# A two-layer graph network with routed experts: routed rows moved into the next layer's staging memory, a fourth load buffer, and turned queries and keys worked out among the values

## The reference, cut to what matters

```python
x = x + gnn0(layernorm(x), src, dst)        # 80000 edges, 4 heads, leaky relu, softmax per target, relu
x = x + moe(layernorm(x))                   # 8 experts, each node goes to its top 2
x = x + gnn1(layernorm(x), src, dst)        # 80000 edges + own loops, 8 heads of 32, then a dense block
x = x + last_layer(layernorm(x))            # routed by the mean, gelu

def moe(tokens):
    rw, re = top_k(softmax(tokens @ router_w.T), 2)
    rw = rw / rw.sum(-1)
    for e in range(8):
        y = gelu(tokens @ w1[e] + b1[e]) @ w2[e] + b2[e]
        out = out + combine[:, e:e + 1] * y      # combine is zero but for the two chosen experts
    return out                                    # starts as tokens

# head of gnn1
Qh = (x @ Wq + bq).reshape(N, 8, 32);  Kh = (x @ Wk + bk).reshape(N, 8, 32)
Vh = (x @ Wv + bv).reshape(N, 8, 32)
s = einsum('nhc,nhc->nh', Qh, Kh) / sqrt(32)      # one score per node and head
```

## Time and profile before

| | |
|---|---|
| Three runs | 2370.11, 2376.10, 2381.61 us (median 2376.10) |
| The profiled execution | 2364.94 us, span 2363.2 us, mean granted TensorE clock 0.844 |
| PE, PEld busy | 1577.8 us (67%), 1284.0 us (54%) |
| DVE busy | 1667.0 us (71%) |
| ACT busy | 826.1 us (35%) |
| POOL busy | 1464.3 us (62%) |
| Four fills of `answered` (page, part 6) | 5632.0 KB each, 45.2 us from issue to landing |
| 27 loads of `sent`, 27 stores of `answered` | 256.0 KB each, 2.7 and 2.0 us |

### The profile page before, as it was taken

How to read it: one execution, slowest core, us unless ns; L and a number is a source line. 1 busy time by engine, 2 the same in 40 slices (tenths; PEclk the granted TensorE clock), 3 DMA queues, 4 the chain that set the end, 5 groups by cost and what they waited for, 6 DMA issues and landing times. The chain is left out here.

```text
span 2363.2 us, 38672 instructions
## 1 busy us (share of the span) xinstructions
PE 1577.8 (67%) x9941; PEld 1284.0 (54%) x10019; DVE 1667.0 (71%) x2748; ACT 826.1 (35%) x2126; POOL 1464.3 (62%) x1570
## 2 busy tenths in 40 slices
PE   4597015788766665377564999404688898758498
PEld 4476014566544444376563777403566666547387
DVE  6688714899755557665563888997578888686676
ACT  4365100000000002455301334106467777525464
POOL 4777747777777773616554777777777777700060
PEclk9799557999887787599786999856899999879799
DMA  5646696666433435333342666764566666430101
GB/s 159 213 139 228 211 404 189 215 208 199 142 106 106 106 106 161 136 121 114 101 130 103 195 213 191 244 194 140 163 217 212 202 217 213 108 100 1 45 10 35
DMA packets 145357, 372.17 MB, mean 157 GB/s; under 512 B 39577, under 2 KB 66473, under 8 KB 131715
## 3 DMA queue, kind: packets, MB, share of 16 engines
q0 software_dynamic: 66144, 180.94, 26.9%
q1 hardware_dynamic: 64447, 161.13, 19.4%
q10 hardware_dynamic: 14692, 29.23, 3.4%
HBM read 262.50 MB, written 108.70 MB: 157 GB/s over the span
## 5 line engine op out<-in xcount | busy, mean ns | idle before, releaser
L1349 DVE TENSOR_TENSOR ms_msg<-e_ring,ms_ps_w 128x1040 f32<-128x1040 f32 (+1 forms) x352 | 437.7, 1244 | 334.7 <-SPq L1267 280.3
L1368 PE MATMUL ms_ps_m<-ms_msg,ms_pick 128*128 128x260 f32 x1408 | 400.2, 441 | 230.6 <-DVE ms_msg L1349 147.3
L893 POOL DMA_INDIRECT e_ring<-table,e_index x465 | 440.2, 947 | 163.0 <-issue 137.1
L1368 PEld LDWEIGHTS ms_ps_m<-ms_msg,ms_pick 128*128 128x128 f32 x1408 | 298.4, 220 | 332.3 <-issue 280.7
L1368 PE MATMUL ms_ps_m<-ms_msg,all_xn 128*128 128x272 f32 x1408 | 364.3, 420 | 89.4 <-issue 71.1
L893 POOL DMA_INDIRECT e_ring<-table,l_index x369 | 353.1, 957 | 114.4 <-issue 111.2
L1368 PEld LDWEIGHTS ms_ps_m<-ms_msg,all_xn 128*128 128x128 f32 x1408 | 273.2, 201 | 180.3 <-issue 126.4
L935 POOL DMA_INDIRECT w_staged<-table,l_stage_index x256 | 267.3, 1044 | 104.6 <-issue 59.2
L768 PE MATMUL sc_ps_e<-sc_keys,sc_hot 125*128 125x100 bf16 (+1 forms) x3840 | 292.0, 230 | 21.3 <-DVE all_xn L713 17.7
L768 PEld LDWEIGHTS sc_ps_e<-sc_keys,sc_hot 125*128 125x128 bf16 x3840 | 256.4, 98 | 68.6 <-DVE all_xn L713 24.9
L671 ACT ACTIVATE sc_rows<-sc_ps_b 125x512 bf16<-125x512 f32 x320 | 173.2, 595 | 294.6 <-remote 171.3
(11 more groups left out here) (497 smaller groups left out, 2793.3 us busy)
## 6 DMA issues: line engine op xcount, KB each, us to landing
...
answered<-l_low_fill ACTq DMA_DIRECT2D x4, 5632.0 KB, 45.2
...
all_acc<-sent SPq DMA_DIRECT2D x27, 256.0 KB, 2.7
answered<-all_acc SPq DMA_DIRECT2D x27, 256.0 KB, 2.0
```

The lines of the kernel that those rows point to most:

```text
L893: pool.indirect_dma_start(out=g.ring[:, slot * QUAD + i // GT, i % GT, :], out_offset=None, in_=s.table[:, :], in_offset=bass.IndirectOffs ...
L1349: dve.tensor_tensor(msg[:, b, :, 0:R].rearrange("p t (h o) -> p t h o", h=H), ring[:, bass.ds(slot, 1), :, :].rearrange("p a t (h o) -> p ...
L1368: mm = pe.matmul(ps_m[b][:, 0:W], pick[:, b, t, :], msg[:, b, t, :], start=t == 0, stop=t == GT - 1)
```

## The change

Four things are changed together.

- `sent` and `answered` are gone. One memory, `s.routed`, takes both, and it is the front part of `s.ahead`, the staging memory. An answer overwrites the rows it was computed from, so the memory needs no zeros: the four fills on ACT and the nine on SP are removed, the wait for the latter too. Regions are `NP` rows apart, and a third row of the table tells where a tile's answer goes.
- There are 4 load buffers instead of 3, and 2 answer buffers instead of 3. The additions of the blocks' own rows (`own_added`) stand ahead of the loop; in the loop only statistics and variance of block 0 remain, and ACT's part of its normalization stands behind the loop. Block 4's return gathers have a buffer and a semaphore of their own.
- Queries and keys are computed turned: the weights' 128 columns are the stationary operand and 512 nodes the moving one, 24 matmuls for a block. ACT adds the query's bias, DVE adds the key's bias and multiplies by the query (2 instructions for a block), and PE sums per head by 8 matmuls with a mask (`of_head`).
- This work is placed block by block among the values, on PE, ACT and DVE. There are three banks for turned rows and two for values in place of four and four. POOL's own code behind the return gathers is unchanged.

```diff
+def staged_rows(s, width):
+
+    quad = P * QUAD * GT * width
+    return s.ahead[0:s.ahead.shape[0] // quad * quad].rearrange("(a p f) -> a p f", p=P, f=QUAD * GT * width)
...
-            if most is None:
-                rows = 8 * SENT_ROWS // ANSWER_FILLS
-                for i in range(ANSWER_FILLS):
-                    into = s.answered[i * rows:(i + 1) * rows, :].rearrange("(p r t) d -> p r (t d)", p=P, t=2)
-                    act.dma_start(into, s.low_fill[:, 0:2 * D].unsqueeze(1).broadcast_to([P, into.shape[1], 2 * D])).then_inc(s.answers_filled, 16)
...
+    DUMMY = X * NP
+    GOT = 4
...
+        got = spare[:, 1024:1024 + GOT * 2 * D].rearrange("p (a t d) -> p a t d", a=GOT, t=2)
+        answer = spare[:, 3072:3072 + 2 * 2 * D].rearrange("p (a t d) -> p a t d", a=2, t=2)
...
+        second_back = [late_back[:, :, :] if b == NB - 1 else back for b in range(NB)]
...
-        turn_banks = [banks[0:2], banks[2:4]]
-        v_banks, qk_banks = banks[4:8], [banks[4], banks[5], banks[6], banks[7]]
...
                     pool.wait_ge(answered, tiles_needed)
-                    if b > BY_POOL:
-                        pool.wait_ge(combined, SUB * b)
+                    back, landed = second_back[b], s.last_returned if b == NB - 1 else returned
...
+                def load(q):
+
+                    row = table_value(ENG.SP, 0, q, DUMMY)
+                    if q >= GOT:
+                        sp.wait_ge(tile_turned, q - GOT + 1)
+                    sp.dma_start(got[:, q % GOT, :, :].rearrange("p t d -> p (t d)"), tile_rows(s.routed, row)).then_inc(got_in[q % GOT], 16)
+
+                def passed(q):
+
+                    sp.wait_ge(stored[q % 2], 16 * (q // 2 + 1))
+                    sp.sem_inc(answered, 1)
+
...
-                sp.dma_start(s.sent[DUMMY:DUMMY + TT, :].rearrange("(p t) d -> p (t d)", t=2), zeros).then_inc(fills_in, 16)
-                sp.wait_ge(held_kept, 1)
...
-                    sp.dma_start(tile_rows(s.sent, count + e * SENT_ROWS), zeros).then_inc(fills_in, 16)
...
-                sp.wait_ge(fills_in, 16 * (X + 1))
                 sp.wait_ge(sent, 16 * 2 * NT)
...
+                for q in range(GOT):
...
-                    if q + 3 < TILES:
-                        load(q + 3)
+                    if q + GOT < TILES:
+                        load(q + GOT)
                     sp.wait_ge(y_kept, q + 1)
                     if q >= 1:
                         passed(q - 1)
-                    sp.dma_start(tile_rows(s.answered, table_value(ENG.SP, 0, q, DUMMY)),
-                                 answer[:, q % 3, :, :].rearrange("p t d -> p (t d)")).then_inc(stored[q % 3], 16)
+                    sp.dma_start(tile_rows(s.routed, table_value(ENG.SP, 2, q, DUMMY + TT)),
+                                 answer[:, q % 2, :, :].rearrange("p t d -> p (t d)")).then_inc(stored[q % 2], 16)
                 passed(TILES - 1)
...
+                        if a >= 2:
+                            pe.wait_ge(v_ready, a - 1)
+                        product(w_v, a, v_banks[a % 2][:, 0:D]).then_inc(v_sum, 1)
+
+                def queries_and_keys(b):
+                    cols = slice(b * TB, (b + 1) * TB)
+                    for f in range(KB):
+                        part = slice(f * P, (f + 1) * P)
+                        for weights, bank, summed, freed in ((w_q, q_bank, q_sum, q_ready), (w_k, k_bank, k_sum, product_ready)):
+                            if b * KB + f >= 1:
+                                pe.wait_ge(freed, b * KB + f)
+                            split_products(pe, bank[:, :], [((weights[0][:, kb, part], weights[1][:, kb, part]), (w.xt[0][:, kb, cols], w.xt[1][:, kb, cols]))
+                                                            for kb in range(KB)]).then_inc(summed, 1)
+
+                def node_scores(b):
+                    pe.wait_ge(product_ready, (b + 1) * KB)
+                    if b >= 1:
+                        pe.wait_ge(score_ready, b)
+                    for q in range(SUB):
+                        for f in range(KB):
+                            first = q * H + f * (H // KB)
+                            dot = pe.matmul(dot_bank[:, first:first + H // KB], qk[:, b % 2, f, q * P:(q + 1) * P], w.of_head[:, :], start=True, stop=True)
+                    dot.then_inc(dot_ready, 1)
...
                 pe.wait_ge(y_kept, TILES)
                 pe.wait_ge(qkv_lows, 3)
                 turn_rows(0)
-                for b in range(NB):
-                    if b + 1 < NB:
-                        turn_rows(b + 1)
-                    values(b)
-                for a in range(NT):
-                    scores(a)
+                turn_rows(1)
+                values(0)
+                queries_and_keys(0)
+                values(1)
+                node_scores(0)
+                turn_rows(2)
+                queries_and_keys(1)
+                values(2)
+                node_scores(1)
+                queries_and_keys(2)
+                turn_rows(3)
+                values(3)
+                node_scores(2)
+                turn_rows(4)
+                queries_and_keys(3)
+                values(4)
+                node_scores(3)
+                queries_and_keys(4)
+                node_scores(4)
 
             @block.scalar
...
                         tile_high_part(q + 2)
                     if q + 1 < TILES:
                         activated(q + 1, expert_of[q + 1])
-                    if q == EARLY_TILE:
-                        deviation2(0)
-                        normalized2(0)
-                deviation2(1)
-                normalized2(1)
-                act.wait_ge(y_kept, TILES)
-                for b in range(NB):
-                    highs(b)
-                    if b + 2 < NB:
-                        deviation2(b + 2)
-                        normalized2(b + 2)
+
+                def queries(b):
+                    for f in range(KB):
+                        act.wait_ge(q_sum, b * KB + f + 1)
+                        if b >= 2:
+                            act.wait_ge(product_ready, (b - 2) * KB + f + 1)
+                        act.activation(query[:, b % 2, f, :], q_bank[:, :], ACT.Identity, bias=w.bias_cols[:, 0, f:f + 1]).then_inc(q_ready, 1)
+
+                def second_norm(b):
+                    deviation2(b)
+                    normalized2(b)
+
+                second_norm(0)
+                second_norm(1)
+                highs(0)
+                highs(1)
+                queries(0)
+                second_norm(2)
+                highs(2)
+                queries(1)
+                queries(2)
+                second_norm(3)
+                highs(3)
+                second_norm(4)
+                queries(3)
+                highs(4)
+                queries(4)
 
             @block.vector
...
+                def add_own(first, end):
+                    for b in range(first, end):
+                        dve.tensor_tensor(s.x[:, blocks[b], :], s.x[:, blocks[b], :], s.xn[:, blocks[b], :], ALU.add).then_inc(own_added, 1)
+
                 expert_of = [w1_low_part(0), w1_low_part(1)]
+                add_own(0, 3)
                 tile_low_part(0)
                 tile_low_part(1)
+                add_own(3, NB)
                 hidden_low_part(0)
...
-                    if q < NB:
-                        dve.tensor_tensor(s.x[:, blocks[q], :], s.x[:, blocks[q], :], s.xn[:, blocks[q], :], ALU.add).then_inc(own_added, 1)
-                    elif q < NB + 3:
-                        qkv_low(q - NB)
+                    if 4 <= q < 7:
+                        qkv_low(q - 4)
                     elif q == EARLY_TILE:
                         dve.wait_ge(combined, SUB)
                         statistics(0, stats2_ready)
                         variance(0, stats2_ready, second_gap)
-                        offsets(0, std2_ready, shift2_ready)
...
+                def products(b):
+                    for f in range(KB):
+                        dve.wait_ge(k_sum, b * KB + f + 1)
+                        dve.wait_ge(q_ready, b * KB + f + 1)
+                        if b >= 2:
+                            dve.wait_ge(dot_ready, b - 1)
+                        dve.scalar_tensor_tensor(out=qk[:, b % 2, f, :], in0=k_bank[:, :], scalar=w.bias_cols[:, 1, f:f + 1], in1=query[:, b % 2, f, :],
+                                                 op0=ALU.add, op1=ALU.mult).then_inc(product_ready, 1)
+
+                def keep_scores(b):
+                    dve.wait_ge(dot_ready, b + 1)
+                    dve.tensor_scalar(score[:, blocks[b], :].rearrange("p a h -> p (a h)"), dot_bank[:, 0:SUB * H], float(O) ** -0.5, None,
+                                      ALU.mult).then_inc(score_ready, 1)
...
+                offsets(0, std2_ready, shift2_ready)
+                for i in range(2):
+                    dve.wait_ge(stored[i], 16 * len(range(i, TILES, 2)))
...
+                norm(1)
+                lows(0)
```

(23 more changed lines are left out.)

172 lines of the change are left out of this document (66 added, 106 removed).

## The result

| | before | changed |
|---|---|---|
| Median | 2381.61 us (11 runs, 2367.91 to 2388.31) | 2359.44 us (11 runs, 2345.37 to 2362.99) |
| Ratio changed / before | | 0.9908, 95% interval 0.9885 to 0.9930 |
| Profiled execution | 2364.94 us, span 2363.2, clock 0.844 | 2352.64 us, span 2350.7, clock 0.839 |
| Last gather of layer 0's message passing | 908.29 | 886.75 |
| First turning of a tile (S) | 1002.21 | 977.84 |

The change made the kernel 22 us faster in the medians (2381.61 - 2359.44; by the interval of the ratio 17 to 27), near the -24 that was forecast; the forecast time was 2352 us, from a median before of 2376.1. The profile shows 26.3 us gained up to the barrier and 12.5 at the end.

What follows compares the result with a forecast made beforehand. POOL's stall of 21.75 us, then its own issues, were taken to bound layer 0's message passing, and a chain the stretch behind the experts' loop; -21.4 - 2 - about 0.5 = -24 gave 2352 us from 2376.1, range 2328 to 2368.

Steps and rivals of the forecast that it cites:

- The fills: Layer 0's message passing: without the four fills on ACT, POOL's stall goes; -21.4 us, bounds -57 and -10.
- The rule on issue times: Skill's rule that initiating a DMA is usually small; by it removing ACT's fills gives nothing, sum -2 instead of -24.
- Start of the loop: Ahead of the experts' tile loop: SP's fill wait goes, first turn at 1001; -1.2 us, between 0 and -2.6.
- The loop: Experts' tile loop: a fourth load buffer issues loads one iteration earlier; iterations 3.45 us, last answer at 1103, bounds 1098 and 1114.
- The way back: POOL's return gathers and combination behind the experts: 27.7 us per block, block 0 from 1039, block 2 through at T + 19.
- T: End of the last answer in the experts' tile loop; 1144.1 before, forecast 1103, 41 us earlier.
- The tail: Behind the loop: interleaved queries and keys lengthen PE's path; rows land at T + 92, 1195 instead of 1196.75, bounds +72 and +104.
- Sum: Whole kernel: -21.4 - 2 - about 0.5 = -24 us, 2341 profiled, 2352 against the median 2376.1.
- Behind the rows: POOL's 24 gathers and 20 scatters after the table's rows land: unchanged at 56.7 us; earlier scores give nothing.
- B: Rival: short tail, PE at full clock, normalizations done beside it; rows at T + 72 to T + 80, 2336 us; chance 0.24.
- C: Rival: small gain, T at 1114, tail at its upper bound or layer 0 giving half; -5 to -13, 2367 us; chance 0.17.
- D: Rival: loop gains nothing because SP's one queue holds loads behind stores; T near 1143, +17, 2393 us; chance 0.05.

Runs made afterwards that it cites:

- scores last: Changed kernel with the turned queries and keys of all blocks behind the last values on PE, ACT and DVE; ratio to before 0.9805.
- normalizations first: Changed kernel, DVE combining and normalizing blocks 3 and 4 once landed, values 3 and 4 ahead of later queries and keys; 2315.71 us, ratio to before 0.9777.
- block 2 on DVE: As the kernel with normalizations first, with block 2 combined by DVE instead of POOL; ratio to before 0.9786.

## Why the prediction was right, point by point

- **The fills.** Forecast -21.4, measured -21.5 at the last gather of the stage. PE's first sums run from 314.71 to 321.2 (forecast: near 323), ahead of POOL's issue at 331.79, so nothing waits. Shown by the stall that comes and goes with the fills (21.75, none, 21.47). The pass ends near 896, as said. The price was read from POOL's wait and not from DVE's 49.5 or ACT's 56.4, and that reading decides the forecast.
- **The rule on issue times.** The prediction set the row against the Trainium skill (DMA: Bandwidth & Descriptors, section Issuing engines are not separate DMA queues). Both hold: a first fill is issued in 0.61 us, "small relative to the DMA itself", which lands after 25.1; of four in a row the later ones took 12.8 to 26.6. The sum by that rule is -2.5 with the prediction's own terms, not the -2 that it gives.
- **Start of the loop.** Forecast -1.2, measured -2.8 (24.37 less 21.54): 1.6 ahead of the last scatter (995.12 to 971.95), 1.2 behind it. Nothing told the parts of the first apart.
- **The loop.** Forecast 102 us, measured 98.6, at the lower bound: 10.8 + 26 x 3.37 is 98.4, and the 97 that the prediction has is its slip. Iterations took 3.29 us instead of 3.37, and the mean clock was 0.96 where the prediction went on from 0.88. Of the 43.3 us gained the fourth load buffer carries 31.2 (129.8 without it) and the moved normalization 2.9; the other 9 were not taken apart.
- **The way back.** Forecast block 0 at S + 38 and block 2 through at T + 19, measured S + 38.2 and T + 24.2 (1100.66): T was 3.4 earlier than forecast, and the first block took 30.9 us instead of 27.7, its first gather at 1.00 and one at 1.39 us, and its eight additions 7.6 us (5.6 in block 2).
- **The tail.** Forecast T + 92, measured T + 94.2. The steps fell as walked: block 1 turned at +8.4 (+9), block 2 at +29.4 (+30), combination 3 at +48.2 (+50.2, from 58.6 less 8.45), block 3 turned at +56.6 (+58.6), block 4 at +74.7 (+74.5). At block 2 two misses cancel: its returns were through at +24.2 and not +19, but it was turned 5.2 us behind them and not 11. The half clock that the prediction puts behind its longer waits is an assumption, and its rows don't show from which wait on it holds; the granted clock was 0.65 from 1100 to 1106 and from 1133 to 1142, behind waits of 5.14 and 9.15 us, and 0.95 from 1087 to 1100.
- **Sum, and luck.** At the rows -26.1 where -21.4 - 2 was said: 1.6 from the start and 3.4 from the loop, less 2.2 in the tail, so part of the closeness is misses that cancel. The forecast let nothing change behind the barrier. There this pair of profiles gives back 13.8 us, within the spread of layer 1, and the medians about 4; that these come so near the forecast is in part luck, as their interval (17 to 27 us) is as wide as half the effect. Of the 7.4 us between 2352 and 2359.44, 5.5 are before's own median, 2381.61 in eleven runs after 2376.10 in three.
- **Behind the rows.** 1227.21 - 1170.67 = 56.5 us, forecast unchanged at 56.7. Scores sooner gave nothing.
- **The rivals.** B asked for the full clock and normalizations beside PE's work; the clock was 0.78, and PE waited 30.2 us in 5 waits for normalized rows. C asked for T + 104, a loop of 113 or half of the fills' 21.4; none came. D asked for a loop that gains nothing. The kernel with three load buffers nearly is it: T in before's time near 1133 and 0.5% (14 us) slower, where D's line gives +7 us.
- **A step that was wrong without harm.** Rival C was discounted because "POOL's blocks, not T, limit part of the tail". The kernel with three load buffers shows the opposite: with T 32 us later the rows came 38.8 later. Behind the loop an order on DVE and PE decides, and not POOL. The forecast held because it walked that order step by step.
- **What the prediction left lying.** It priced the interleaved queries and keys as part of a tail of 92 and went no further. They cost 19 us, and with combinations in order of landing 23 were to be had.

The cause of layer 1's spread (1099 to 1119 us for the same code) stays open. In the changed kernel's profile one gather of POOL accounts for 8.8 us of it, and from 1561 us to its end the trace has no DMA traffic:

```profile
1559.11 9.73 POOL L934 DMA_INDIRECT w_staged<-table,l_stage_index  x1 [0.30 <-issue]
```

DVE ran L1150 and L1151 back to back over nearly the same time (1559.12 to 1568.02). In scores last, normalizations first and block 2 on DVE the gathers beside these instructions took at most 1.19 us, so whether they held POOL here isn't shown.
